# A graph network layer on one core: the first 128 edge groups placed from small transfers, the rest of the placing moved behind the sums of tiles 0 and 1

## What is computed

```python
h = jnp.maximum(_layernorm(x, axis=-1), 0.0)
# L0_gnn_ref(h, edge_attr, (src, dst), W1 .. b3):
agg_edge = jax.ops.segment_sum(edge_attr, dst, num_segments=12500)
collected = jnp.concatenate([h, agg_edge], axis=1)      # 128 + 48
z = jax.nn.silu(collected @ W1 + b1)                    # 256
z = jax.nn.silu(z @ W2 + b2)                            # 256
delta_u = z @ W3 + b3                                   # 128
out = x + (h + delta_u)
```

## Time and profile before

| | |
|---|---|
| median of 3 runs | 367.52 us (366.28 to 370.0) |
| profiled execution | 369.57 us, of which the span from the first to the last instruction is 367.8 us |
| PE busy / DVE / ACT / POOL | 94% / 71% / 55% / 9% of the span |
| instructions | 11,752 |
| moved | 52.96 MB, 144 GB/s on average |
| mean granted clock of TensorE | 0.989 of 2.4 GHz |

### The profile page before, as it was taken

How to read it: one execution, slowest core, us unless ns; L and a number is a source line. 1 busy time by engine, 2 the same in 40 slices (tenths; PEclk the granted TensorE clock), 3 DMA queues, 4 the chain that set the end, 5 groups by cost and what they waited for, 6 DMA issues and landing times.

```text
span 367.8 us, 11752 instructions
## 1 busy us (share of the span) xinstructions
PE 347.2 (94%) x4336; PEld 327.8 (89%) x4337; DVE 260.8 (71%) x630; ACT 203.1 (55%) x377; POOL 32.6 (9%) x44
## 2 busy tenths in 40 slices
PE   1488999999999999999999999999999999999995
PEld 1387999999999999999999999999999999999994
DVE  6864866976687667866796669766876688666652
ACT  7543466555655566456645565556555654566471
POOL 4011101110111001110111011101110011101100
PEclk9996999999999999999999999999999999999999
DMA  4953756454555455455635554545554555551111
GB/s 136 295 158 83 219 152 177 131 167 134 175 134 165 127 173 168 131 138 172 182 115 152 165 174 123 169 133 175 137 163 127 172 153 149 138 170 28 27 27 47
DMA packets 78757, 52.96 MB, mean 144 GB/s; under 512 B 2482, under 2 KB 78348, under 8 KB 78738
## 3 DMA queue, kind: packets, MB, share of 16 engines
q1 hardware_dynamic: 78738, 52.70, 50.3%
HBM read 46.29 MB, written 6.40 MB: 143 GB/s over the span
## 4 chain that ended last, share of the span: by engine, by line
PE 93%; DVE 4%; issue 2%; POOL 1%; ACTq 0%; DVEq 0%; POOLq 0%; ACT 0%
PE agg_ps L836 41%; PE z L899 14%; PE z L880 7%; PE z L888 6%; PE z L882 6%; PE z L869 3%; PE z L864 3%; PE z L870 3%; PE z L865 3%; PE z L866 3%; PE tp L849 3%; DVE farthest L522 1%; PE z L774 1%; DVE window L505 0%; DVE rel_rows L518 0%
## 5 line engine op out<-in xcount | busy, mean ns | idle before, releaser
L836 PEld LDWEIGHTS agg_ps<-onehot,raw 128*48 128x48 f32 x3128 | 147.8, 128 | 7.3 <-issue 3.6
L836 PE MATMUL agg_ps<-onehot,raw 128*48 128x42 f32 x3128 | 151.1, 217 | 3.3 <-issue 3.3
L714 DVE TENSOR_TENSOR out_t<-z,resid 112x512 f32<-112x512 f32 (+1 forms) x28 | 19.4, 692 | 84.6 <-PE z L899 84.6
L558 DVE TENSOR_TENSOR onehot<-window,rel 128x1176 f32<-128x1176 f32 (+1 forms) x56 | 76.9, 1375 | 0.7
L425 ACT ACTIVATE xn<-x_t,nmr,rstd 112x128 f32<-112x128 f32 (+1 forms) x112 | 46.2, 483 | 36.6 <-DVE nmr L550 29.8
L899 PEld LDWEIGHTS z<-w,h 128*112 128x112 f32 (+1 forms) x448 | 51.7, 176 | 5.3 <-issue 4.5
L377 POOL TENSOR_TENSOR rstd<-vareps,minus_half 112x4 f32<-112x4 f32 (+1 forms) x28 | 28.2, 1008 | 312.0 <-DVE vareps L542 312.0
L899 PE MATMUL z<-w,h 128*112 128x128 f32 (+1 forms) x448 | 54.4, 274 | 0.9 <-ACT h L446 0.9
L446 ACT ACTIVATE h<-z,b2c 128x448 f32<-128x448 f32 (+1 forms) x56 | 32.4, 631 | 26.5 <-PE z L888 26.5
L880 PE MATMUL z<-h_hi,w_hi 128*128 128x448 f32 (+1 forms) x112 | 43.5, 389 | 0.0
L385 ACT ACTIVATE agg_ps<-zeros 48x512 f32<-48x512 f32 x28 | 16.5, 592 | 45.4 <-DVE agg_carry L668 45.4
(11 more groups left out here) (89 smaller groups left out, 341.4 us busy)
## 6 DMA issues: line engine op xcount, KB each, us to landing
raw<-in_edge_attr_dram SPq DMA_DIRECT2D x55, 672.0 KB, 4.6
x_t<-in_x_dram SPq DMA_DIRECT2D x27, 224.0 KB, 2.9
out_dram<-out_t SPq DMA_DIRECT2D x27, 224.0 KB, 2.5
dst_rows<-in_dst_dram SPq DMA_DIRECT2D x1, 768.0 KB
raw<-in_edge_attr_dram SPq DMA_DIRECT2D x1, 480.0 KB, 4.0
out_t<-in_L_gnn_W_dram SPq DMA_DIRECT2D x1, 256.0 KB, 7.0
x_t<-in_x_dram SPq DMA_DIRECT2D x1, 192.0 KB
out_dram<-out_t SPq DMA_DIRECT2D x1, 192.0 KB
```

Of the source, the lines that this page charges most:

```text
L558: return dve.tensor_tensor(onehot[:, slot, 0:n * PER, :], window[:, :].unsqueeze(1).broadcast_to([P, n * PER, WINDOW]), cols.unsqueeze(2). ...
L836: mm = pe.matmul(banks[0:ED, bass.ds(offsets[k], WINDOW)], raw[0:rows, slot, k, j, :], onehot[0:rows, slot, k * PER + j, :], start=False, ...
```

## The change

Seven edits, all in the part before the loop reaches its second step:

1. SP first issues small transfers: the first target of each group alone (`first_i`, 384 + 6 + 1 numbers of 4 bytes) and row 0 of `dst_rows` (128 groups, 256 KB). The first edges follow without a wait, the other rows of `dst` behind them; the weights, the constants and the edges of tile 1 are put in another order, and the edges of tile 2 are issued before SP reads the flag.
2. The index arithmetic is rewritten: what needs only the expected position is done before `dst` comes, offsets follow from the distance to that position.
3. Row 0 (128 groups, the tiles 0 to 8) is placed alone; its offsets go to PE by one matmul. An invalid group of row 0 gets targets far outside the window, so that its sums add nothing until the branch.
4. The transposes of rows 1 to 3 come behind the sums of tile 0; the other offsets, the count of invalid groups and the branch come behind 11 of the 14 groups of tile 1 and the transposes of tile 0. Step 0 of the loop is written out by hand around them, on all engines.
5. POOL makes fewer constants at first, and waits for the offsets of row 0 before the larger memsets.
6. ACT clears `agg_carry` in four pieces instead of three, the last behind `hT_hi` of tile 0.
7. PE runs matmuls whose result nobody reads: 10 of 128 columns while it waits for row 0, and 12 of 42 columns and 4 of 128 behind the transposes of row 0.

The diff, cut to its core:

```diff
-        ACT_ZEROS = (POOL_ZEROS, 16 * TILE, 22 * TILE, NT * TILE + OVER)
+        ACT_ZEROS = (POOL_ZEROS, 10 * TILE, 15 * TILE, 21 * TILE, NT * TILE + OVER)
...
@@ sync @@
-            sp.wait_ge(s_dst, 64)
-            for half in range(2):
-                load_edges(0, 0, half)
+            sp.dma_start(first_i[:, 0:FULL_ROWS], rows[:, :, 0], allow_slow_non_contiguous=True).then_inc(s_first, 16)
+            sp.dma_start(dst_rows[:, 0, :], rows[:, 0, :]).then_inc(s_dst0, 16)
...
+            load_edges(0, 0, 0)
+            sp.dma_start(dst_rows[:, 1:FULL_ROWS, :], rows[:, 1:FULL_ROWS, :]).then_inc(s_dst, 16)
...
+            load_edges(0, 0, 1)
             load_x(0, 0)
+            load_edges(1, 1, 0)
...
@@ gpsimd @@
+            pool.wait_ge(s_small0, 1)
+            pool.memset(agg_hilo[:, :].bitcast(F32), 0.0).then_inc(s_pool_zero, 1)
+            pool.memset(w1e_hi[:, :].bitcast(F32), 0.0).then_inc(s_pool_zero, 1)
+            pool.memset(w1e_lo[:, :].bitcast(F32), 0.0).then_inc(s_pool_zero, 1)
+            pool.iota(tile_i[:, :], pattern=[[1, TILE]], base=0, channel_multiplier=0).then_inc(s_pool_zero, 1)
             pool.memset(agg_carry[:, 0:POOL_ZEROS], 0.0).then_inc(s_carry0, 1)
...
@@ scalar @@
+            rel_of(0)
             clear_carry(1)
-            act.wait_ge(s_const, CONSTS)
+            clear_carry(2)
+            for c in range(1, ROWS):
+                rel_of(c)
+            act.wait_ge(s_weights, WEIGHTS)
...
@@ vector @@
+            dve.scalar_tensor_tensor(g["placed"][:, 0:1], g["moved3"][:, 0:1], g["valid"][:, 0:1],
+                                     g["at_centre"][:, 0:1], ALU.mult, ALU.add).then_inc(s_small0, 1)
+            link(dve.tensor_scalar(g["far"][:, 0:1], g["valid"][:, 0:1], -FAR, FAR, ALU.mult, ALU.add))
+            dve.tensor_scalar(rel_rows[:, 0, :], rel_rows[:, 0, :], g["far"][:, 0:1], None,
+                              ALU.add).then_inc(s_relrow, 1)
...
+            dve.wait_ge(s_small0T, 1)
+            dve.tensor_copy(offset_row[:, 0:P], z3[0:1, 0, :]).then_inc(s_off0, 1)
             dve.wait_ge(s_rel, 1)
             make_onehot(0, 0, 0)
+            make_onehot(0, 0, 1)
+            dve.wait_ge(s_dst, 64)
+            for c in range(1, ROWS):
+                rows_of(c)
+            make_onehot(1, 1, 0)
+            load_stats(0, 0)
...
@@ tensor @@
+            for _ in range(WARM0):
+                pe.matmul(tp[:, 0:P], ident[:, :], ident[:, :], start=True, stop=True)
+            pe.wait_ge(s_small0, 1)
+            pe.matmul(z3[0:1, 0, :], g["placed"][:, 0:1], ident[:, :], start=True, stop=True).then_inc(s_small0T, 1)
+            turn_rows(0)
+            for k in range(WARM1):
+                pe.matmul(tp[0:ED, 0:WINDOW], ident[:, 0:ED], ident[:, 0:WINDOW], start=True, stop=True)
...
+            pe.wait_ge(s_off0, 1)
+            offsets = offsets_of(0)
+            sum_tile(0, 0, offsets)
+            offsets = offsets_of(1)
+            for c in range(1, ROWS):
+                turn_rows(c)
+            sum_groups(1, 1, 0, offsets[0:HALF])
+            sum_groups(1, 1, 1, offsets[HALF:], 0, HALF - EARLY)
+            transposes(0, 0)
...
+            where_invalid(pe, mybir.EngineType.PE, general_path)
+            sum_groups(1, 1, 1, offsets[HALF:], HALF - EARLY, HALF)
             pipeline(pe, step)
```

More of the change, by code:

```diff
@@ L113, in gnn_kernel @@
         centre_i = sb("centre_i", [P, ROWS], I32)
+        first_i = sb("first_i", [P, ROWS], I32)
         g = {n: sb("g_" + n, [P, ROWS]) for n in (
-            "base", "middle", "centre", "drift", "ok1", "ok2", "ok3", "valid", "invalid",
-            "tile", "tilet", "tile_half", "pair", "parity", "offset", "offset2", "offset3",
-            "at_centre", "instead", "placed", "shift")}
+            "base", "middle", "minus_middle", "centre", "tilet", "tile", "tile_half", "pair", "parity",
+            "begin", "in_tile", "at_centre", "other", "if_before", "if_behind", "from_centre",
+            "drift", "place", "before", "behind", "moved1", "moved2", "moved3", "ok1", "ok2", "ok3",
+            "valid", "invalid", "far", "chosen", "placed", "shift")}
         rel = sb("rel", [P, NG, PER])
@@ L237, in pipeline @@
         def pipeline(eng, step):
-            for i in range(LOOP_FIRST):
+            for i in range(1, LOOP_FIRST):
                 step(i, i % 2)
@@ new lines, in _ @@
+            link(dve.tensor_scalar(g["tile"][:, :], g["tilet"][:, :], MAGIC, -MAGIC, ALU.add, ALU.add))
+            link(dve.tensor_scalar(g["tile_half"][:, :], g["tile"][:, :], 0.5, -0.25, ALU.mult, ALU.add),
+                 dve.tensor_scalar(g["begin"][:, :], g["tile"][:, :], float(TILE), None, ALU.mult))
+            link(dve.tensor_scalar(g["pair"][:, :], g["tile_half"][:, :], MAGIC, -MAGIC, ALU.add, ALU.add),
+                 dve.tensor_tensor(g["in_tile"][:, :], g["centre"][:, :], g["begin"][:, :], ALU.subtract))
@@ new lines, in _ @@
+            row_sets = ((P, slice(0, FULL_ROWS)), (LAST_G, slice(FULL_ROWS, ROWS)))
+            dve.wait_ge(s_first, 48)
+            link(*[dve.tensor_copy(g["base"][0:r, c], first_i[0:r, c]) for r, c in row_sets])
+            link(dve.tensor_scalar(g["middle"][:, :], g["base"][:, :], REACH, None, ALU.add),
+                 dve.tensor_tensor(g["drift"][:, :], g["base"][:, :], g["centre"][:, :], ALU.subtract),
+                 dve.tensor_tensor(g["place"][:, :], g["base"][:, :], g["begin"][:, :], ALU.subtract))
@@ L582, in _, with weights_lo @@
-            dve.tensor_tensor(g["placed"][:, :], g["offset3"][:, :], g["instead"][:, :], ALU.add).then_inc(s_small, 1)
+            def weights_lo():
+                dve.wait_ge(s_w_hi, 4)
+                dve.wait_ge(s_pool_zero, 4)
+                for lo, whole, hi in (
+                        (w2_lo[:, :, :].rearrange("p m n -> p (m n)"), w2_in.rearrange("p m n -> p (m n)"),
+                         w2_hi[:, :, :].rearrange("p m n -> p (m n)")),
+                        (w1x_lo[:, :], w1x_in, w1x_hi[:, :]),
+                        (w1e_lo[0:ED, :], w1e_in[0:ED, :], w1e_hi[0:ED, :])):
+                    dve.tensor_tensor(lo, whole, hi.bitcast(F32), ALU.subtract).then_inc(s_w_lo, 1)
```

245 lines of the change are left out of this document (132 added, 113 removed).

## The result

| | before | after |
|---|---|---|
| median of 20 runs | 366.99 us (366.28 to 370.0) | 369.82 us (367.17 to 370.76) |
| ratio after / before | | 1.0057, interval 1.0039 to 1.0075 |
| profiled execution | 369.57 us, span 367.8 | 368.25 us, span 366.5 |
| PE / DVE / ACT / POOL busy | 94% / 71% / 55% / 9% | 96% / 71% / 55% / 9% |
| mean granted clock | 0.989 | 0.985 |

The change makes the kernel slower, by 0.4 to 0.75%; forecast was a gain of 2.7 us. The two profiled executions alone say the opposite (367.8 against 366.5), and that is the first lesson of this case. One trace of this kernel is one draw out of a spread of four us. One execution of the kernel before and one of the kernel with the flag first and the residual early took some 1,900 us; the ratios leave them out.

What follows compares the result with a forecast made beforehand. PE sets the pace in the unchanged steady part, so only the start could gain. Its steps moved tile 1's transposes from 39.99 to 37.3; the 2.7 us off the median of 367.52 gave 364.8 us, range 361.0 to 368.2.

Steps and rivals of the forecast that it cites:

- The pass over row 0 (`far`): DVE's chain for row 0: placed at 7.4, second pass done at 8.0, 8.3 with the rest of a POOL memset.
- the sign I had named for being wrong on the clock: Sums of tile 0: 49 passes in 2 us at 12 would make the forecast wrong on the clock.
- The small transfers: Landing of the first targets and row 0 of `dst`: row 0 at 4.7, 1.2 us earlier than all of `dst`.
- Behind the branch on DVE: After the flag's branch at 30.7: statistics of tile 1, then `agg` to `hT_lo`, 2.7 us; layer 1 at 33.4 against 37.75.
- PE's last three groups run beside what follows: Tile 1's last three groups on PE, behind the branch, were taken to overlap the following work; no time was added.
- the 2.8 us of ACT's last piece: ACT's `agg_carry` piece of 3200 columns: 2.8 us, from 27.9 to 30.7, ahead of `agg`.
- Layer 1 to the transposes: Layer 1 of tile 0 up to tile 1's transposes: 3.4 us, likely starting at the lower level, against 2.24 before.
- the 0.5 us that I had for the lower level in tile 2's sums: Sums of tile 2 on PE: 0.5 us more, counted with layer 1's 3.4 to put the transposes at 37.3.
- Upper level throughout: Rival: idle matmuls lift PE's clock and waits don't lower it; transposes at 33.7, gain 6.3, 361.2 us; chance 0.25.
- Lower level throughout: Rival: PE at the lower clock from start to layer 1; 5.3 us later than before, 372.8 us; chance 0.05.
- POOL holds DVE: Rival: row 0's second pass waits for five POOL operations, ending at 11.4; first sum 2.8 later, 367.6 us; chance 0.12.
- Small transfers don't help: Rival: the first targets land as late as all of `dst` did; 1.3 us of the gain gone, 366.1 us; chance 0.08.

Runs made afterwards that it cites:

- the kernel with the flag first and the residual early: The kernel with the flag early, with DVE's flag read behind tile 1's second table and tile 0's residual ahead of tile 2's first table: 364.28 us, ratio 0.9908.
- statistics early: The change with tile 1's statistics on DVE ahead of the offsets' copy and the flag instead of behind the branch: 370.13 us, ratio 1.005.
- without the flag: The change without flag reads, branches and general path, the copy of rows 1 to 3's offsets behind the carry's low part: 370.19 us, ratio 1.0039.
- ACT's piece and the statistics early: The change with tile 1's statistics ahead of the flag and ACT's last `agg_carry` piece ahead of the copies of rows 1 to 3: 368.29 us, ratio 1.0028.
- ACT's piece early, without the flag: The change without flag, branch and general path, and with ACT's last `agg_carry` piece ahead of the copies of rows 1 to 3: 363.66 us, ratio 0.9885.
- the kernel with the flag early: The change with rows 1 to 3's offsets, count, flag and branch directly behind tile 0's sums, all `agg_carry` pieces early: 366.01 us, ratio 0.9945.

## Why the prediction was wrong, step by step

**The early steps held.** The pass over row 0 (`far`) ended at 8.46 against 8.3 forecast, the first sum came at 11.55 in 11.3 to 13.0, tile 0 ended at 16.78 against 18.1 since the upper level held from its first pass (49 passes at 12, the sign I had named for being wrong on the clock), the register wait was 2.46, the flag was read at 28.75 against 29.6. The small transfers brought what they were counted for.

**The step that failed is "Behind the branch on DVE",** and in it the sentence "PE's last three groups run beside what follows". They can't: they need the bank that ACT clears behind DVE's carry, and the carry stands behind the branch. Of the whole chain, branch to `agg` to carry to cleared bank to 24 passes to layer 1, the sum had only the network's side (statistics and `agg` to `hT_lo`, 2.7 us), and that side was ready at 32.24, 1.9 us before layer 1 could start. I had the second gate in the text, the 2.8 us of ACT's last piece "ahead of `agg`", and priced it at nothing because it ended at the flag's time. Two waits that end together are worth nothing to the one who removes either, and the full price to the one who removes both. That is shown by four runs: statistics early 370.13 (ACT's piece held), without the flag 370.19 (the same), ACT's piece and the statistics early with the flag kept 368.29 (the flag held), and both away 363.66. The traces show it without the spread of the times, by the stretch from the end of the eleven groups to the start of the last three:

| kernel | eleven groups end | last three start | between |
|---|---|---|---|
| the change | 26.48 | 31.98 | 5.50 |
| statistics early | 27.28 | 32.78 | 5.50 |
| without the flag | 28.46 | 33.96 | 5.50 |
| ACT's piece and the statistics early | 28.22 | 32.92 | 4.70 |
| ACT's piece early, without the flag | 28.36 | 30.09 | 1.73 |

The change once more, the change without idle matmuls and the change with its offsets moved have 5.50, 5.51 and 5.50 too, whatever the clock had done before. With both gates away PE's wait falls from 3.98 to 0.20 us and the time by some 6 us. The table has 3.8 of the six; a part of the rest is that PE, no longer standing, has the upper level for the 24 passes (1.27 us instead of 2.15) and through layer 1.

On the clock of the trace it took 5.4 us from the flag's read (28.75) to layer 1 (34.12), where I had 3.8 (29.6 to 33.4). Only 0.7 of these 1.6 show at layer 1, since what stands ahead of the flag was 0.85 early. Layer 1 to the transposes took 3.92 us against 3.4 counted, at PEclk 0.53, but the 0.5 us that I had for the lower level in tile 2's sums didn't come (5.17). So the transposes are at 38.04 against 37.3.

**The larger error is the reference.** The 2.7 us were the distance from 39.99, a start that belongs to a trace 2.05 us above its median, and I laid them on that median. Against the second trace of the kernel before (36.80) my own 37.3 is a loss of 0.5, and the measured 38.04 one of 1.2. That trace in turn is 0.8 under the median of its spans, so for a median execution I estimate the transposes at 36.80 + 0.8 = 37.6, from which 37.3 would have been a gain of 0.3. I had seen the 2.05 and asked only how to carry the gain over, not what in the first 40 us had made that execution long. The rows held the hint: 7.93 and 7.40 us of sums in the earlier trace rows where the steady ones take 5.16. That is 5.0 us lost to the lower level, and in the second trace it is 3.1 (6.73 and 6.66). The Trainium skill (TensorE: Matmul & The Clock Gate, Part 1) says that the count of matmuls at the lower level varies between runs of one kernel. The traces agree: tile 0's sums of the unchanged program took 7.93 and 6.73 us.

**What is not accounted for.** The traces give the change 0.7 to 1.2 us at the transposes and 0.9 to 1.7 in the span; the medians give it 2.0 to 2.8. Some of it has a place: from tile 3's sums to the end the change's traces take 316.1 and 315.9 us, those of before 315.5 and 315.6, so the part that I had expected to stay as it is lost 0.3 to 0.6, spread over the tiles and without a cause that a run shows. Another 0.1 lies outside the span: time less span is 1.85 and 1.83 in the medians of the change's two sets of runs, 1.71 in that of the kernel before. Of the change's 32 executions 15 have a span over 368.0 us; of the kernel before six of 35 reach 367.9. No trace of the change is from those, so what is longer in them isn't shown. The trace without the flag (368.5) suggests the lower level from the eleven groups to layer 1. What the move by 8 bytes gave beyond the half microsecond behind tile 3 is open for the same reason.

**The rivals.** *Upper level throughout* had its first half: it came for tile 0 (first sum to 16.78 against the rival's 16.5) and was lost behind the first wait. *Lower level throughout* was the side on which the time ended, with another mechanism. Its price was a loss of 5.3; what came was the wait on the bank with the lower level behind it. *POOL holds DVE*: the pass took 1.03 us, just over the 1 us I had named. DVE's pass began with POOL's first memset (7.46, 0.47 us) and ended at 8.46, far ahead of the end of the fifth (11.06). The first subtraction over row 0, the same size, took 0.49, so by my estimate the mechanism cost 1.03 - 0.49, about 0.5 us, and not 3. *Small transfers don't help* was wrong: the first targets had landed at 4.36, and `farthest` of row 0 began at 5.78, where the earlier trace rows have 8.90.

## What to carry to other kernels

Before a gain is counted from a trace, see where that trace stands among the runs, and which of its terms make it long or short; what a long execution alone had to lose can't be taken off the median. When a branch or a wait is moved, write down everything that becomes ready behind it and who waits for that, and count two gates that end together as one, which must be opened together. An earlier start is worth what the next chain in order leaves of it: here ten us of it became one lost.

## What the runs showed of the hardware

*Register loads by their start.* Fourteen numbers take 1.34 us or 3.4 us, by whether they start at a multiple of 16 bytes from the row's start; moving them by 8 bytes swapped which load is long, and the wait behind tile 0 fell from 2.46 to 0.46 us. *Idle matmuls ahead of a register load delay it.* The load of tile 1's offsets starts at 15.8 in the change, 1.0 us before tile 0's sums end, and at 18.0 with eleven idle matmuls ahead of it, 0.5 us after they end. The time between the sums is 3.93 and 3.95 us instead of 2.46 in two kernels. *POOL beside a table.* `rstd`, four numbers for each partition, takes 1.01 us at 31.79 and 2.02 at 16.62, beside DVE's two-input table (2.03 in the kernel with the flag early). The Trainium skill (SBUF — State Buffer, Who interferes with whom) says that a DVE instruction with two SBUF inputs contends with a GpSimd instruction that reads SBUF; these rows agree. Only POOL paid here, the table itself staying at 1.38.
